# V's projection in a float32 attention block: high and low half of Wv in one 512-column matmul, the halves added on evacuation

## The reference

```
proj(x, W) = einsum('bsd,ed->bse', x, W)      # q, k, v: Wq, Wk, Wv are 1024 x 1024
q = q * min(cond, 4)
attn = softmax(causal(q k^T / 8))
out  = (attn v) Wo^T
x + absmax_int8(out) @ ternary(weight)^T + bias
```

## Time and profile before

| | |
|---|---|
| median of 3 runs | 2095.14 us (2094.16 to 2096.12) |
| profiled execution | 2099.02 us, its span 2097.2 us |
| busy: PE, PEld, DVE, ACT, POOL | 98%, 82%, 61%, 48%, 39% |
| granted TensorE clock, mean | 0.994 of full speed (2.4 GHz) |
| DMA queues | 29% of 16 engines |
| attention steps, feed-forward part | about 0 to 1600 us, 1600 to 2097 us |

### The profile page before, as it was taken

One profiled execution on the slowest core, in us unless ns is written; L12 is line 12 of the kernel. 1 busy time (PEld: TensorE's weight loads), 2 busy tenths in 40 slices (PEclk: granted clock), 3 DMA queues, 4 the chain that ended last, 5 costly groups with the idle time before them and its releaser, 6 DMA issues.

```text
span 2097.2 us, 38177 instructions
## 1 busy us (share of the span) xinstructions
PE 2046.0 (98%) x11745; PEld 1729.4 (82%) x11776; DVE 1279.0 (61%) x3163; ACT 1012.0 (48%) x2383; POOL 807.8 (39%) x746
## 2 busy tenths in 40 slices
PE   8999999999999999999999999999977999999998
PEld 7888888888888888888888888888866777777776
DVE  5666666766666666666665766666658554545454
ACT  5566565656555656565565655655565000000000
POOL 3433333433333334433333433333334544444442
PEclk9999999999999999999999999999989999999999
DMA  4222224222222322222223222222244423232322
GB/s 161 71 82 96 71 75 141 71 71 70 77 78 70 130 72 71 71 82 95 72 75 132 81 71 70 70 78 77 90 146 141 141 95 119 91 120 90 120 90 80
DMA packets 85932, 194.42 MB, mean 93 GB/s; under 512 B 7392, under 2 KB 40160, under 8 KB 84320
## 3 DMA queue, kind: packets, MB, share of 16 engines
q1 hardware_dynamic: 85856, 193.50, 29.0%
HBM read 126.36 MB, written 33.55 MB: 76 GB/s over the span
## 4 chain that ended last, share of the span: by engine, by line
issue 49%; PE 24%; POOL 22%; DVE 2%; DMA 1%; POOLq 1%; ACT 1%; SPq 0%; DVEq 0%; ACTq 0%
POOL prob L283 17%; PE s_ps L560 8%; PE proj_ps L560 8%; POOL parts L373 5%; PE o_ps L631 5%; PE proj_ps L169 2%; PE t_ps L609 1%; DMA w_raw<-wf 1%; POOLq L282 1%; DVE parts L511 0%; DMA x_raw<-xT 0%; DVE w_raw L484 0%; DVE w_raw L486 0%; DVE prob L264 0%; PE t_ps L293 0%
## 5 line engine op out<-in xcount | busy, mean ns | idle before, releaser
L169 PE MATMUL proj_ps<-parts 128*128 128x512 f32 (+1 forms) x6144 | 1224.3, 347 | 16.9 <-DVE parts L373 12.3
L169 PEld LDWEIGHTS proj_ps<-parts 128*128 128x128 f32 x6144 | 934.7, 190 | 130.2 <-issue 13.3
L283 POOL TENSOR_TENSOR prob<-prob,row_inv 128x128 f32<-128x128 f32 (+3 forms) x512 | 396.4, 777 | 953.8 <-DVE row_inv L277 942.9
L264 DVE CUSTOM_DVE_ANT_0 prob<-s_ps,mask 128x128 f32<-128x128 f32 (+3 forms) x512 | 250.0, 488 | 355.4 <-PE t_ps L293 197.2
L307 ACT ACTIVATE pt_hi<-t_ps 128x128 fp32r<-128x128 f32 (+3 forms) x512 | 222.5, 435 | 441.5 <-PE t_ps L293 432.6
L271 ACT ACTIVATE prob<-prob,row_min 128x128 f32<-128x128 f32 (+3 forms) x512 | 286.4, 559 | 85.2 <-DVE row_min L264 78.8
L314 DVE TENSOR_TENSOR pt_lo<-t_ps,pt_hi 128x128 fp32r<-128x128 f32 (+3 forms) x512 | 249.5, 487 | 75.0 <-ACT pt_hi L307 69.5
L293 PE MATMUL t_ps<-ident,prob 128*128 128x128 f32 x1280 | 229.1, 277 | 22.2 <-POOL prob L283 20.2
L616 ACT ACTIVATE yt_q<-t_ps 128x1024 bf16<-128x1024 bf16 x32 | 32.8, 1024 | 428.0 <-PE t_ps L609 428.0
L373 POOL TENSOR_TENSOR parts<-x_raw,parts 128x512 fp32r<-128x512 f32 x128 | 202.4, 1601 | 56.1 <-ACT parts L369 56.1
L293 PEld LDWEIGHTS t_ps<-ident,prob 128*128 128x128 f32 x1280 | 152.0, 141 | 47.6 <-POOL prob L283 21.6
(11 more groups left out here) (63 smaller groups left out, 1905.4 us busy)
## 6 DMA issues: line engine op xcount, KB each, us to landing
x_raw<-xT SPq DMA_DIRECT2D x128, 512.0 KB, 5.9
k_sw<-k_st SPq DMA_DIRECT2D x128, 256.0 KB, 3.8
oT_scratch<-o_sum SPq DMA_DIRECT2D x64, 256.0 KB, 2.6
x_raw<-oT_scratch SPq DMA_DIRECT2D x32, 512.0 KB, 4.8
x_tile<-x SPq DMA_DIRECT2D x32, 512.0 KB, 5.6
out<-res SPq DMA_DIRECT2D x32, 512.0 KB, 3.1
w_raw<-wf SPq DMA_DIRECT2D x16, 512.0 KB, 4.5
w_raw<-wq SPq DMA_DIRECT2D x4, 1024.0 KB, 6.4
```

What stands on the lines that cost most here:

```text
L169: mm = pe.matmul(out, l, r, start=(k == 0 and i == 0), stop=(k == KT - 1 and i == 2))
L264: dve.tensor_tensor_reduce(prob[:, u % 4, 0:w], s_ps[u % 2][:, 0:w], mask[:, S - w:S], 1.0, -MASKED, ALU.add, ALU.min, row_min[:, u % 4:u ...
L283: pool.tensor_tensor(prob[:, u % 4, 0:w], prob[:, u % 4, 0:w], row_inv[:, u % 4:u % 4 + 1].broadcast_to([P, w]), ALU.mult).then_inc(norm_d ...
```

## The change

Wv's high and low part are laid out in turns (slice by slice), so that 512 neighbouring columns hold both. Per slice, one matmul with x's high part streams all 512 into the whole bank: the first half gets high x high, the second half high x low. A second matmul adds x's low part times Wv's high part into the first half. Two matmuls of 512 and 256 columns stand where three of 256 were. The bank then holds two addends, and the evacuation has four links: ACT copies the second half to SBUF (`v_cross`), DVE adds the first half to it (`v_add`) in a new tile `v_sum` with two slots, ACT makes the high part from `v_sum` (`evac_hi`), DVE the low part (`evac_lo`). TensorE's wait for the bank stays at `proj_lo_done`.

```diff
         w_part = [parts[:, i * WP:(i + 1) * WP].rearrange("p (k e) -> p k e", e=EG) for i in range(6)]
-        w_hi, w_lo = w_part[0::2], w_part[1::2]
+
+        wv_both = parts[:, 4 * WP:6 * WP].rearrange("p (k a e) -> p k a e", a=2, e=EG)
+        w_hi, w_lo = w_part[0:4:2] + [wv_both[:, :, 0, :]], w_part[1:4:2] + [wv_both[:, :, 1, :]]
...
+        v_sum = sb("v_sum", [P, 2, EG], F32, one_ctx)
...
             if kind == "v":
                 tok = slice(n * P, (n + 1) * P)
-                out = bank[:, 0:EG]
-                passes = [(x_lo[:, k, tok], w_hi[w][:, k, :]), (x_hi[:, k, tok], w_lo[w][:, k, :]),
-                          (x_hi[:, k, tok], w_hi[w][:, k, :])]
+                pe.matmul(bank[:, :], x_hi[:, k, tok], wv_both[:, k, :, :].rearrange("p a e -> p (a e)"),
+                          start=(k == 0), stop=False)
+                mm = pe.matmul(bank[:, 0:EG], x_lo[:, k, tok], w_hi[w][:, k, :], start=False, stop=(k == KT - 1))
...
+        def v_cross(act, it, gi):
+            n = groups[gi][1]
+            proj_ready(act, it, gi)
+            if due(count := it * NEV + EVAC[gi] - 2 if n >= 2 else (it - 1) * NEV + EVAC[gi + 2]):
+                act.wait_ge(proj_lo_done, count)
+            act.activation(v_sum[:, n % 2, :], proj_ps[gi % 2][:, EG:2 * EG], ACT.Copy).then_inc(v_cross_done, 1)
+
+        def v_add(dve, it, gi):
+            n = groups[gi][1]
+            dve.wait_ge(v_cross_done, it * QT + n + 1)
+            dve.tensor_tensor(v_sum[:, n % 2, :], proj_ps[gi % 2][:, 0:EG], v_sum[:, n % 2, :], ALU.add)\
+               .then_inc(v_sum_done, 1)
...
-            proj_ready(act, it, gi)
+            if kind == "v":
+                act.wait_ge(v_sum_done, it * QT + n + 1)
+            else:
+                proj_ready(act, it, gi)
             if kind == "v":
                 if n == 0:
                     if due(count := it * HG):
                         act.wait_ge(pv_done, count)
-                act.activation(v_view(n, 0), bank[:, 0:EG].rearrange("p (h d) -> p h d", d=DH),
+                act.activation(v_view(n, 0), v_sum[:, n % 2, :].rearrange("p (h d) -> p h d", d=DH),
                                ACT.Copy).then_inc(proj_hi_done, 1)
...
-                dve.tensor_tensor(v_view(n, 1), bank[:, 0:EG].rearrange("p (h d) -> p h d", d=DH),
+                dve.tensor_tensor(v_view(n, 1), v_sum[:, n % 2, :].rearrange("p (h d) -> p h d", d=DH),
                                   v_view(n, 0).bitcast(F32), ALU.subtract).then_inc(proj_lo_done, 1)
```

More of the change, by code:

```diff
@@ L120, in adaln_ffn_kernel @@
         proj_done = sem("proj_done")
+        v_cross_done = sem("v_cross_done")
+        v_sum_done = sem("v_sum_done")
         proj_hi_done = sem("proj_hi_done")
@@ L159, in project @@
                 tok = slice(n * P, (n + 1) * P)
-                out = bank[:, 0:EG]
-                passes = [(x_lo[:, k, tok], w_hi[w][:, k, :]), (x_hi[:, k, tok], w_lo[w][:, k, :]),
-                          (x_hi[:, k, tok], w_hi[w][:, k, :])]
+                pe.matmul(bank[:, :], x_hi[:, k, tok], wv_both[:, k, :, :].rearrange("p a e -> p (a e)"),
+                          start=(k == 0), stop=False)
+                mm = pe.matmul(bank[:, 0:EG], x_lo[:, k, tok], w_hi[w][:, k, :], start=False, stop=(k == KT - 1))
             else:
                 col = slice(n * P, (n + 1) * P)
-                out = bank[:, :]
                 passes = [(w_lo[w][:, k, col], x_hi[:, k, :]), (w_hi[w][:, k, col], x_lo[:, k, :]),
                           (w_hi[w][:, k, col], x_hi[:, k, :])]
-            for i, (l, r) in enumerate(passes):
-                mm = pe.matmul(out, l, r, start=(k == 0 and i == 0), stop=(k == KT - 1 and i == 2))
+                for i, (l, r) in enumerate(passes):
+                    mm = pe.matmul(bank[:, :], l, r, start=(k == 0 and i == 0), stop=(k == KT - 1 and i == 2))
             if gi == NPROJ - 1:
@@ L815, in V, with VB @@
                     evac_hi(act, n, gi)
+            def VB(gi):
+                if now:
+                    v_cross(act, n, gi)
             def OL(h):
@@ L847, in act_step @@
             if old:
-                evac_hi(act, o, 7)
+                v_cross(act, o, 7)
             if ending:
@@ L851, in act_step @@
             E(7)
+            if old:
+                evac_hi(act, o, 7)
             if ending:
@@ L903, in act_step @@
             H(1)
-            V(4)
+            VB(4)
             if last and now:
@@ L907, in act_step @@
             E(3)
+            V(4)
             W(2)
@@ L912, in act_step @@
                 wo_high(act, 2)
-            V(5)
+            VB(5)
             W(3)
             H(3)
+            V(5)
             E(5)
@@ L918, in act_step @@
                 wo_high(act, 3)
-            V(6)
+            VB(6)
             X(0)
             H(4)
+            V(6)
             X(1)
@@ L950, in V, with VA @@
                     evac_lo(dve, n, gi)
+            def VA(gi):
+                if now:
+                    v_add(dve, n, gi)
             def OA(h):
@@ L975, in dve_step @@
             if old:
-                evac_lo(dve, o, 7)
+                v_add(dve, o, 7)
             L(5)
             I(7)
+            if old:
+                evac_lo(dve, o, 7)
             if ending:
@@ L1051, in dve_step @@
             L(1)
-            V(4)
+            VA(4)
             I(3)
@@ L1063, in dve_step @@
                 wo_low(dve, 2)
+            VA(5)
+            M(5)
             V(5)
-            M(5)
             W(3)
@@ L1072, in dve_step @@
             M(6)
-            V(6)
+            VA(6)
             if nxt:
```

## The result

The changed kernel takes 2158.38 us (median of 4 runs, 2157.65 to 2159.88), the kernel before 2094.65 us (4 runs, 2093.34 to 2096.12). The ratio is 1.0305 with an interval of 1.0291 to 1.0319: slower by 63.7 us. The profiled execution took 2158.81 us, its span 2157.0.

The account below looks back on a forecast made before the run. TensorE, busy 2046.0 of 2097.2 us, was taken as the bound. Terms 19.6 + 6.6 + 2 + 29.1 + 3.1 - 6.0 = 54.4 us on 2095.1 gave about 2150 us; range 2116 to 2176, 8 in 10.

Parts of the forecast that it names:

- both waits: Likeliest case: TensorE is delayed by the late bank release and by the late x split; 65%, range 2136 to 2166 us.
- term 2: Change of step: ACT splits the next x 0.94 us late, behind V group 6's upper part; 29.1 us over 31 changes.
- Merge: V's projection matmuls: one of 512 columns saves 7.8 ns against two of 256; 8.0 us, of which 6.0 remain.
- Term 1: Mid-step: the first matmul of V group 6 waits for group 4's lower part; 0.7 us, 19.6 in 28 ordinary steps.
- J(7,0) is safe: First matmul of V group 7: group 5's evacuation is done before it is due; nothing to 0.05 us.
- the 0.94 therefore goes straight to TensorE: Change of step: POOL's x-lower chain has no gap, so the late x split delays TensorE fully; bounds 0.6 and 1.2 us.
- one wait is covered: Rival: only the bank wait or only the change-of-step waits cost time; 2115 or 2121 us, 15%.
- Term 3: Change of step: V group 7's late lower part delays PV's first matmul; 0.1 us each, 3.1 in 31, bounds 0 to 0.4.
- An ordinary step: Sum for one step without weight splits, not the last: 0.7 + 0.94 + 0.1 - 0.2, 1.5 us longer.
- Steps 7, 15, 23: Steps where DVE also splits weights: V group 6's first matmul waits longer for group 4's lower part; 3 x 2.2 = 6.6 us.
- Last step: Final step: the same bank wait, partly hidden by TensorE's existing wait for feed-forward weights; 2 us, between 0 and 5.
- POOL slows too: Rival: V's subtractions with both operands in SBUF slow POOL's x-lower chain; 25 us more, 2175 us, 11%.

Follow-up runs that it names:

- the early release: Changed kernel, but TensorE's wait for a V group's bank is for DVE's add instead of V's lower part: 2125.20 us.
- the last version: Changed kernel with the sum in PSUM, V evacuations mostly moved early, and DVE's first x-lower part ahead of group 6's add: 2093.36 us, 0.9992 of the kernel before.

## Why the prediction was right, and where its sizes were off

The case was the likeliest one (both waits), and 2158.4 lies in its own range. That it lies there is in part luck: term 2 came out under the 0.75 us at which that range starts, and the steps with splits and the last step well over their sizes, and this cancels in part. By its steps:

- **Merge: 7.8 ns per pair.** Shown by the merge alone: 0.23 us in 32 pairs on TensorE's side, 7 ns, of which POOL's chain takes back 0.08. Net 5.2 us; the sum had 6.0.
- **Term 1, ordinary step: 0.7.** Measured 0.69, and shown by the early release (back to 2.71) and by moving V(4).
- **J(7,0) is safe.** Right: TensorE has no wait there in the ordinary step.
- **Term 2: 0.94.** The mechanism holds: X(1) is 0.97 late, and with the sum in PSUM the move of V(6) behind X(1) brings the change of step from 5.35 to 4.80. The size was too large. From T(6) to J(0,3) the trace has 661.16 - 660.04 = 1.12 us, before 638.63 - 638.16 = 0.47: 0.65. The failed step is "the 0.94 therefore goes straight to TensorE". Starting late, POOL's x-lower(1) at 656.89 misses DVE's x-lower(0), beside which it began before (633.99), and takes 1.29 in place of 1.67 us, so POOL regains 0.38. The prediction had this in its bound of 0.6 and named it for the rival in which one wait is covered, but gave it no place in the sum. DVE's x-lower(0) before and after:

```profile
633.81 0.68 DVE L373 TENSOR_TENSOR parts<-x_raw,parts 128x512 fp32r<-128x512 f32 x1
655.75 0.68 DVE L393 TENSOR_TENSOR parts<-x_raw,parts 128x512 fp32r<-128x512 f32 x1
```

- **Term 3: 0.1.** Too small: the rest of the change of step, 1.10 - 0.65 = 0.45 us. The stretch from J(0,3) to PV(0) grew from 1.52 to 2.18 us, and the first matmul behind that wait cost 0.09 more. "The wait of T(7) behind it swallows most" held only for 0.29 of this 0.75 (J(0,5) to T(7): 1.28 us before, 0.99 after), for T(7) had no more to give. V(7)'s subtraction took 0.62 instead of 0.42. The experiments divide the 1.10 us in much the same way: 0.25 goes when the sum is in PSUM (5.60 to 5.35), 0.55 when V(6) stands behind X(1) (to 4.80), 0.23 when V(7) is early (to 4.57), and the last 0.07 are there with the merge alone too.
- **An ordinary step: +1.5.** Measured +1.55, but as 0.69 + 0.65 + 0.45 - 0.24: terms 2 and 3 erred in opposite directions.
- **Steps 7, 15, 23: 3 x 2.2.** Measured 3 x 3.8: such a step grew by 53.43 - 48.77 = 4.66 us, less the 0.86 of terms 2, 3 and the gain. The wait was sized right: where V(6) was moved behind X(1), the same wait of 1.95 us passed with the clock at full, and T(2) to T(3) was 4.91 us, 2.17 longer. The other 1.6 us are two things that the prediction did not have, and the clock is the smaller. With the clock at 0.51, T(2) to T(3) grew to 5.40 to 5.54 us and T(3) to T(4) from 2.93 us to between 3.82 and 4.00, some 1.6 us together. But in every run with an added chain in which the clock held in such a step, TensorE stands once more between T(5) and T(6), at J(0,0) or J(0,1): 3.85 to 4.57 us where the kernel before has 2.83 and the changed one 2.81. The slower TensorE of the changed kernel comes too late to meet that wait. One kernel shows both, the run of V(6) with the sum in PSUM: its steps 7 and 23 kept the clock and took 52.01 and 52.03 us, its step 15 lost it behind a wait of the same length and took 52.57. So the clock as such cost some 0.55 us, and the wait about 1 (for the changed kernel an estimate, from that run). That run's rows at J(6,0) in steps 7 and 15, the windows behind them, and J(0,0) in step 7:

```profile
391.29 0.50 PE L165 MATMUL proj_ps<-parts 128*128 128x512 f32 x1 [1.92 <-DVE v_st L243]
792.61 0.50 PE L165 MATMUL proj_ps<-parts 128*128 128x512 f32 x1 [1.91 <-DVE v_st L243]
391.30:394.70 3.40, 3.40 (x21) 3.09 (x22) 1.31 (x6) 2.24 (x5) 0.40 (x1) 1.00 0.01 2
793.60:796.90 3.30, 3.30 (x13) 2.98 (x13) 0.93 (x4) 1.36 (x4) 0.00 (x0) 0.50 0.01 2
399.76 0.50 PE L173 MATMUL proj_ps<-parts 128*128 128x512 f32 x1 [0.77 <-DVE v_st L243]
```

- **Last step: 2, from 0 to 5.** Measured 6.15. TensorE stands 5.05 us, because L(2) comes as late as before and V(4)'s lower part now stands behind it. "TensorE already waits for DVE's feed-forward weights there" was a wrong reading. Between T(2) and T(4) of the last step of before it has these two waits, T(3) for POOL's N(3) and J(7,0) for V(5)'s lower part, and both lie behind J(6,0):

```profile
1582.77 0.66 PE L293 MATMUL t_ps<-ident,prob 128*128 128x128 f32 x4 [0.83 <-POOL prob L283]
1586.77 0.62 PE L169 MATMUL proj_ps<-parts 128*128 128x256 f32 x3 [1.56 <-DVE v_st L223]
```

They cover only part: T(2) to T(3) grew from 3.97 to 9.12 us, T(3) to T(4) shrank from 4.80 to 3.82. The stretch from T(6) to T(7), in which PV(0) waits 3.3 us for V(7)'s lower part (the longest of the waits of L349 above), took 2.4 more. The 2 us were a choice between far ends without a row, and the wrong one.

The spans differ by 59.8 us; the sum had 54.4. The steps with splits add 4.8 to it and the last step 4.1. The three changes of step at which the loop's code changes (behind steps 14, 22, 30) grew by 1.6 us together instead of 3 x 1.55, which is most of the other sign. The medians differ by 3.9 us more than the spans: the profiled execution of before lies 4.4 us over its median, that of the changed kernel 0.4. The prediction named that distance.

The rival "POOL slows too" did not come in the size given to it (2175 us). V(6)'s subtraction starts at 656.61, 0.28 us ahead of POOL's x-lower(1), since X(1) is late too, and neither is longer for it. But the contention is there, at 0.27 us per step in the changed kernel, and at 0.84, with DVE as the one that stands, once the places are mended.

**Open.** Why the last version keeps a residue of about 3 us over the merge alone is told in part only: 3 x 1.4 us in the split steps and 1.25 in the last step are seen in the trace, less 2.5 us in the changes of loop code; an order without them was not found. Why the changes of loop code differ by up to 5 us from kernel to kernel was not tried. What decides whether TensorE's clock falls behind a standstill of 1.9 us stays open: standstills of one length had both outcomes.

## What to carry to other kernels

A longer evacuation chain costs little as work (some 100 us of instructions on two engines with room cost an ordinary step nothing here) and much as places: ask for each link who waits for it and what stands queued behind it, and let the bank's reuse wait for the last reader of the bank, not for the last link. In lists written by hand a link that needs another engine's answer must not stand ahead of the work that feeds the slackless chain. And weigh the gain first: merging two equal-moving passes saved 7 to 8 ns per pair, 5 us in 2095, so one wait of 0.2 us per step eats it.
